# A fused cross-attention and ternary-FFN kernel: one pair's transposes gathered, gate, up and down gathered, and the FFN transpose bank moved

## The reference

```
x = x + softmax(mask(LN(x) Wq (ctx Wk)^T / 8)) (ctx Wv) Wo + bo
h = act_quant(LN(x));  gate = silu(h Wg^T);  up = h Wu^T      # 128 -> 512
x = x + act_quant(gate * up) Wd^T                             # 512 -> 128
act_quant: per row, scale = 127 / max|row|, round, clip, / scale
weights: round(w / mean|w|) clipped to -1..1, times mean|w|
```

## Time and profile before

| what | value |
|---|---|
| median of 3 runs | 822.8 us (821.91 to 822.95) |
| the profiled execution's own time | 821.9 us |
| its span | 820.1 us |
| PE busy | 783.2 us (96%), 5487 records |
| DVE busy | 678.8 us (83%) |
| ACT busy | 678.9 us (83%) |
| POOL busy | 407.3 us (50%) |
| chain that ended last | PE 81%, DVE 8%, issue 5%, ACT 4% |

### The profile page before, as it was taken

One profiled execution on the slowest core, in us unless ns is written; L12 is line 12 of the kernel. 1 busy time (PEld: TensorE's weight loads), 2 busy tenths in 40 slices (PEclk: granted clock), 3 DMA queues, 4 the chain that ended last, 5 costly groups with the idle time before them and its releaser, 6 DMA issues.

```text
span 820.1 us, 17819 instructions
## 1 busy us (share of the span) xinstructions
PE 783.2 (96%) x5487; PEld 542.6 (66%) x5550; DVE 678.8 (83%) x1845; ACT 678.9 (83%) x1202; POOL 407.3 (50%) x404
## 2 busy tenths in 40 slices
PE   7899999999999999999999999999999999999983
PEld 5667666766766766676666676676676667666552
DVE  7749888888878887988888888788888888878894
ACT  4688888888888887988888888788888888888882
POOL 1235555454554545555545545555454554544551
PEclk9999999999999999999999999999999999999997
DMA  7100010100101000010100101010010100000000
GB/s 225 53 1 1 15 38 16 39 2 14 40 14 39 13 18 22 13 39 13 38 2 13 39 13 38 14 39 0 13 39 14 39 13 13 1 14 15 1 14 14
DMA packets 37109, 20.50 MB, mean 25 GB/s; under 512 B 1460, under 2 KB 36534, under 8 KB 37046
## 3 DMA queue, kind: packets, MB, share of 16 engines
q1 hardware_dynamic: 37046, 19.84, 8.3%
HBM read 15.64 MB, written 4.19 MB: 24 GB/s over the span
## 4 chain that ended last, share of the span: by engine, by line
PE 81%; DVE 8%; issue 5%; ACT 4%; POOL 1%; DMA 0%; DVEq 0%; POOLq 0%; ACTq 0%
PE ps_s L431 13%; PE ps_a L500 12%; PE ps_s L402 5%; PE ps_s L322 4%; PE ps_kv L402 3%; PE ps_kv L322 3%; PE ps_s L324 3%; PE ps_kv L323 3%; PE ps_s L323 3%; PE ps_s L404 3%; PE ps_b L459 3%; PE ps_s L403 3%; PE ps_a L459 3%; PE ps_kv L403 3%; PE ps_kv L324 3%
## 5 line engine op out<-in xcount | busy, mean ns | idle before, releaser
L872 POOL TENSOR_TENSOR prob<-prob,row_max 128x1024 f32<-128x1024 f32 x64 | 122.0, 1906 | 189.4 <-DVE row_max L747 189.4
L520 ACT ACTIVATE vp<-ps_s 64x512 f32<-64x512 f32 x256 | 151.2, 590 | 33.2 <-PE ps_s L404 28.9
L890 POOL TENSOR_TENSOR prob<-prob,row_rec 128x512 f32<-128x512 f32 x128 | 130.9, 1044 | 56.3 <-DVE row_rec L822 56.3
L520 ACT ACTIVATE vp<-ps_kv 64x512 f32<-64x512 f32 x256 | 151.5, 592 | 5.4
L882 POOL TENSOR_TENSOR hid_b<-hid_q,neg_round 128x512 bf16<-128x512 f32 x64 | 66.7, 1041 | 128.1 <-DVE hid_q L791 128.1
L500 PE MATMUL ps_a<-vp,prob_t 128*64 128x128 f32 x2048 | 125.9, 276 | 1.3 <-DVE x L769 1.2
L431 PE MATMUL ps_s<-kp,xn_t 128*64 128x512 f32 x512 | 124.0, 605 | 2.9 <-ACT vp L520 1.9
L500 PEld LDWEIGHTS ps_a<-vp,prob_t 128*64 128x64 f32 x2048 | 110.6, 137 | 24.4 <-issue 16.3
L744 DVE TENSOR_TENSOR prob<-ps_s,bias_sb 128x1024 f32<-128x1024 f32 x64 | 78.3, 1223 | 54.3 <-PE ps_s L431 53.7
L520 ACT ACTIVATE kp<-ps_s 128x512 f32<-128x512 f32 x130 | 77.8, 599 | 11.9 <-PE ps_s L290 8.2
L849 POOL TENSOR_TENSOR rs<-ve,neg_half 128x1 f32<-128x1 f32 x128 | 70.4, 550 | 33.1 <-DVE ve L669 24.5
(11 more groups left out here) (175 smaller groups left out, 1725.5 us busy)
## 6 DMA issues: line engine op xcount, KB each, us to landing
x_in<-in_x SPq DMA_DIRECT2D x16, 256.0 KB, 2.9
ctx_in<-in_ctx SPq DMA_DIRECT2D x16, 256.0 KB, 3.4
x_res<-in_x SPq DMA_DIRECT2D x16, 256.0 KB, 2.8
out<-x SPq DMA_DIRECT2D x15, 256.0 KB, 2.4
kp<-in_L_xattn_Wk SPq DMA_DIRECT2D x1, 512.0 KB, 4.0
kp<-in_L_xattn_Wq SPq DMA_DIRECT2D x1, 512.0 KB, 4.9
kp<-in_L_xattn_Wv SPq DMA_DIRECT2D x1, 512.0 KB, 6.1
kp<-in_L_xattn_Wo SPq DMA_DIRECT2D x1, 512.0 KB, 6.1
```

The source lines that it names most:

```text
L520: copy = lambda dst, src, **kw: nc.scalar.activation(dst, src, ACT.Copy, **kw)
L872: p.tensor_tensor(prob[c % 2][:], prob[c % 2][:], rows(row_max[c % 2]), ALU.subtract).then_inc(shifted, 1)
L890: p.tensor_tensor(prob[c % 2][:, heads, :], prob[c % 2][:, heads, :], rows(row_rec[c % 2])[:, heads, :], ALU.mult).then_inc(normed, 1)
```

## The change

`ps_h`, where the hidden row is transposed, becomes half of the bank of gate (`ps_g`) and no longer half of `ps_b`. On TensorE both halves of the probability transposes stand directly behind the scores and the other transposes. Then comes the first V' unit (where it wasn't placed early), then gate, up and down, then the K' unit. ACT follows: the copy of the second half of the probabilities now stands ahead of tanh, and where q = 0 and there is a next group the two copies of the first V' unit stand ahead of it too. The numbers of matmuls, copies and bytes stay as they are. DVE, POOL and SP are untouched.

```diff
-        ps_h = ps_b[:, 0:F // 2].bitcast(BF16)
+        ps_h = ps_g[:, 0:F // 2].bitcast(BF16)
@@ TensorE, slot
                     prob_transposes(0, ps_a)
+                    pe.wait_ge(normed, 2 * s)
+                    prob_transposes(1, ps_b)
+                if not early:
+                    v_quarter(0)
                 if live(it, c, 2):
                     pe.wait_ge(xqt_evac, s - 1)
+                    if live(it, c, 3):
+                        pe.wait_ge(ht_evac, s - 2)
                     mm(ps_g[:, :], xq_t[:], wg_t[:], ...).then_inc(gate_ready, 1)
                     mm(ps_u[:, :], xq_t[:], wu_t[:], ...).then_inc(up_ready, 1)
-                if not early:
-                    v_quarter(0)
-                if live(it, c, 1):
-                    pe.wait_ge(normed, 2 * s)
-                    if live(it, c, 3):
-                        pe.wait_ge(ht_evac, s - 2)
-                    prob_transposes(1, ps_b)
-                k_quarter(0)
                 if live(it, c, 3):
                     ...                                  # down, unchanged
+                k_quarter(0)
                 v_quarter(1)
@@ ScalarE, slot
                 take_probs(0, ps_a)
+                if group_ahead(it, c, 1) and q == 0:
+                    take_v(0)
+                take_probs(1, ps_b)
                 if live(it, c, 2):
                     ...                                  # tanh, unchanged
-                if group_ahead(it, c, 1):
-                    take_v(0)
-                    take_probs(1, ps_b)
-                else:
-                    take_probs(1, ps_b)
+                if not (group_ahead(it, c, 1) and q == 0):
                     take_v(0)
```

## The result

The changed kernel takes 843.29 us (median of 4 runs, 842.79 to 844.13) against 822.88 us (821.91 to 822.98): ratio 1.0252, 95% interval 1.0234 to 1.0270. It is slower by 20.4 us, where 20.7 were added up in the prediction. The profiled execution took 843.35 us, with a span of 841.6 where it had been 820.1.

A forecast was written before the change was run, and what follows sets the result against it. TensorE was taken to bound the ordinary slot. Terms 14.3 + 2.2 + 4.2 = 20.7 us on the profiled execution's 821.9 gave 842.6, or 843.5 at the median; forecast 843 us, 8 in 10 within 833 to 851.

The forecast's parts named there:

- Slots with q = 0: In 14 slots, tanh behind the V' copies delays DVE's last sum and so attention: net 1.02 us each, 14.3 us.
- the give-back: Where q = 0, the third K' unit's 0.29 us wait for ACT's copy vanishes under attention's delay.
- Ordinary slots: In 44 other slots, later tanh moves the K' copies and so the third K' unit: 0.05 us each, 2.2 us.
- ACT follows about 0.04 later: In ordinary slots, tanh on ACT starts about 0.04 us after gate ends on TensorE.
- Last group and tail: Without K' units the slots lengthen: 3.0 us in three slots plus 0.6 twice, 4.2 us, ends 2 and 6.
- The loop from `xq` to `xq`: In the last group, the chain through DVE, TensorE and ACT takes 10.61 us, 0.99 more per slot.
- 0.16 us for POOL: In the last group's loop, the second transposes wait for POOL's second half, signal included: 0.16 us added.
- two thirds of the loop: The last group's first slot and the first tail slot lose two thirds of a loop slot's loss: 0.6 us each.
- TensorE's order: Fewer changes of type between neighbours on TensorE gain 0.02 us a slot, some 1 us, hidden by later waits.
- Rival A: Gathering pays on TensorE: up to 0.11 us per change of type, three a slot, 20 us back: 823 or 815; chance 0.07.
- B: Where q = 0, attention doesn't wait, so only 2.2 + 4.2 remain: 829 us; chance 0.07.
- C: POOL becomes the bound: its second half arrives late, 44 slots each lose 0.25 us: 854 us; chance 0.05.

The follow-up runs named there:

- act_order_alone: The kernel before, with only ACT's new order where q = 0 (V' copies, second probabilities, then tanh): 834.8 us, ratio 1.0164.
- tanh_before_v: The changed kernel, with ACT copying both halves of the probabilities, then tanh, then the first V' copies in every slot: 831.29 us, ratio 1.0145.
- attention_in_ps_b: The changed kernel, with the attention product written to `ps_b` and no wait for DVE's last sum (L767): 838.36 us, ratio 1.0212.
- before_k_first: The kernel before, with ACT's copy of the second K' unit ahead of the exponential where q = 0: 818.83 us, ratio 0.9964.
- k_copy_before_exp: The changed kernel, with ACT's copy of the second K' unit ahead of the exponential in every slot: 840.43 us, ratio 1.0232.
- after_all_three: The changed kernel with tanh_before_v, k_copy_before_exp and attention_in_ps_b together: 822.84 us, ratio 1.0018 against the kernel before.

## Why the prediction was right, point by point

**Slots with q = 0: 14.3 us predicted, 14.1 measured.** The chain was right link by link. Tanh starts 2.20 us behind the first copy of probabilities, as worked out (0.48 + 1.23 + 0.49); L767 starts 0.98 behind `gated` (0.99); attention's weights have 1.61 us of idle time where 0.36 is normal, a wait of 1.25 (1.31), and the K' wait gives its 0.29 back. What remains is 0.98 (1.02) in each plain slot. act_order_alone and tanh_before_v show the cause from both sides, attention_in_ps_b the link from L767, before_k_first the give-back. The signal from DVE was 0.12 and not 0.15. The slots are not equal: 1.03 to 1.21, 1.15 in the mean, at the five loop-body starts, and 0.5 in slot 56, whose DVE has no first layer norm left to do. I had them all at 1.02, and the differences cancel.

**Ordinary slots: 2.2 us predicted, 3.4 measured.** The mechanism was right, and k_copy_before_exp shows it: tanh, then V' copies, then the K' copy, then the third K' unit. The step that was mis-sized is ACT's start behind gate, "ACT follows about 0.04 later". It was 0.04 outside the loop and 0.12 inside (gate's end from attention_in_ps_b, which has this order and gate's records, and the same distance from up's start, 0.20 and 0.28, in the changed kernel), so 36 slots lose 0.09 each and the six others 0.01 to 0.02. The range of -0.02 to +0.15 held it. The trace of before could not show the size: there ACT wasn't waiting at tanh in an ordinary slot.

**Last group and tail: 4.2 us predicted, 3.3 measured.** The loop from `xq` to `xq` was right as a mechanism, and three of its terms were off. Two were too large. I had 0.16 us for POOL, but the second transposes start at 789.44, 0.05 behind POOL's end at 789.39 and 0.47 behind the first ones, that is 0.03 later than four transposes need. And `gated` follows tanh by 0.03 there, not 0.11. One was too small: up starts 1.43 behind the second transposes (789.44 to 790.87), where an ordinary slot has 1.36. With these three the loop's 10.61 becomes 10.47, and the rows say 10.47. The first period of the group rose by 0.61 (0.6 predicted), but not as two thirds of the loop, which is how I had it: attention_in_ps_b brings it to 9.52 while the loop's periods stay at 10.48, so it was attention's wait for L767, and the 0.6 was luck. The second rose by 0.71 only. In the tail luck helped the sum. Up to the last sum on DVE it lost 2.3 us, and 1.1 only because what lies behind that sum was 1.2 shorter than before, which the change doesn't explain: two kernels with the old order have 2.0 there as well. Without that stroke this term would read 4.5.

**TensorE's order: 0.02 us a slot, hidden.** The size is 0.02 to 0.04, and hidden it was, until k_copy_before_exp uncovered it. The argument for it was weaker than it looked: the 0.70 of a unit was itself worked out from rows that hold such a change of type, so those rows couldn't show what a change costs. Rival A (0.3 a slot) is refuted by the runs: after_all_three, where neither attention nor the third K' unit waits as in the changed kernel, saves 0.02 and not 0.3.

**The other rivals.** B fell with attention's wait. C, POOL, never came: no wait of the second transposes for POOL stands in the waits of after, and only in the last group do they start 0.03 late. D fell with the granted clock of 1.00 over the eight gathered transposes, the 2.4 GHz level. The Trainium skill ("TensorE: Matmul & The Clock Gate", Part 4: PE-mode transpose) has the full clock not engage for transposes; in this kernel, with dense matmuls on both sides of them, the trace disagrees.

**The sum.** 14.1 + 3.4 + 3.3 makes 20.8 of the span's 21.5; setup and the first four slots have 0.7, most of it noise. One term was low by 1.2 and one high by 0.9, the latter only through the shorter end, so 843 is nearer to 843.3 than its terms deserve.

## What to carry to other kernels

When a change groups work on one engine, follow what the other engines must now do first: here, where TensorE was the bound, gathering its work won or cost no more than 0.04 us a slot, while two copies put ahead of tanh on ACT cost 1.0. In the last group, where a loop through three engines was the bound, the four transposes and their copy, ahead of gate and tanh, cost 0.5 a period. Look for an instruction whose successor on another engine has a slack smaller than the move, and for what that successor guards (here a shared bank). And ask of a wait that your sum gives back whether it can be had by itself: swapping two ACT instructions took 3 us off the kernel that was there before.

## What the hardware showed that I had not expected

- The same instruction, idle at its wait, starts at different lags behind the matmul that frees it: tanh 0.20 us behind up's start outside the loop, 0.28 inside, and 0.26 or 0.27 in both with the two waits exchanged. In 36 slots the 0.08 make 2.9 us. The cause is open.
- `gated` follows the end of tanh by 0.11 in the loop's ordinary slots (421.76 to 421.87) and by 0.03 in the last group (791.76 to 791.79), though DVE is idle for it in both. The 0.03 stands from slot 56 on and at the start of each loop body too. The cause is open.
- The bracket of a wait for several semaphores misled in the very row that mattered: attention was put down to "issue" and to a V' copy that ended just ahead of it but that it doesn't wait for, while the end of L767 stood 0.12 us ahead. The code says which counts an instruction waits for, and attention_in_ps_b settled it.
